# Interleaving the first two pairs of chunks and re-timing the queues of an AdaLN-conditioned FFN kernel

## The reference, cut to what matters

```python
def lora_add(base, inp, A, B):          # A, B chosen per sequence
    t = einsum('bri,bni->bnr', A[idx], inp)
    return base + einsum('bor,bnr->bno', B[idx], t) * 0.5
gate = lora_add(x @ W_gate.T, x, A_gate, B_gate)      # 1024 -> 2752
up   = lora_add(x @ W_up.T,   x, A_up,   B_up)
act  = silu(gate) * up
y    = lora_add(act @ W_down.T, act, A_down, B_down)  # 2752 -> 1024
logits = y @ Wg + bg                                  # 8 experts
top2 = top_k(logits, 2)
out = x + mean over the two experts e of relu(y @ W_e[e] + b_e[e])
```

## Time and profile before

| | us |
|---|---|
| median of three runs | 2058.62 |
| profiled execution, its own time | 2062.44 |
| its span from first to last instruction | 2060.6 |
| TensorE busy | 1882.0 |
| DVE, POOL, ACT busy | 1141.9, 1083.1, 744.0 |
| mean granted TensorE clock | 0.954 |

### The profile page before, as it was taken

How to read it: one execution, slowest core, us unless ns; L and a number is a source line. 1 busy time by engine, 2 the same in 40 slices (tenths; PEclk the granted TensorE clock), 3 DMA queues, 4 the chain that set the end, 5 groups by cost and what they waited for, 6 DMA issues and landing times.

```text
span 2060.6 us, 24701 instructions
## 1 busy us (share of the span) xinstructions
PE 1882.0 (91%) x8679; PEld 1560.7 (76%) x8679; DVE 1141.9 (55%) x1355; ACT 744.0 (36%) x1054; POOL 1083.1 (53%) x659
## 2 busy tenths in 40 slices
PE   4789998999798996799999999798989999999997
PEld 3567776778687785688888888687867788888886
DVE  6446766566358675356666666349684744443210
ACT  4333433334344332444444434333331233333332
POOL 5357877674244443245555545144441666666664
PEclk8899999999899998899999999899998899999999
DMA  4256766653457553323343334456563476666653
GB/s 161 81 169 208 239 251 238 239 182 106 161 183 249 197 195 117 118 92 113 100 135 114 113 101 130 152 199 236 199 203 109 145 195 181 182 179 155 156 111 61
DMA packets 118025, 332.67 MB, mean 161 GB/s; under 512 B 13952, under 2 KB 15872, under 8 KB 117760
## 3 DMA queue, kind: packets, MB, share of 16 engines
q1 hardware_dynamic: 99632, 268.06, 37.5%
q0 software_dynamic: 18272, 62.99, 13.1%
HBM read 249.86 MB, written 90.05 MB: 165 GB/s over the span
## 4 chain that ended last, share of the span: by engine, by line
PE 66%; DVE 7%; issue 6%; DMA 6%; POOL 5%; ACT 3%; SPq 0%; ACTq 0%; DVEq 0%; POOLq 0%
PE PS L1571 20%; PE PS L1572 19%; PE PS L1573 19%; DVE FT L1205 3%; DMA brw<-in_bgu,idx_b 3%; PE PS L1878 2%; PE PS L1616 2%; PE PS L1710 1%; DMA ytp<-in_wgb 1%; POOL brw L691 1%; DMA raw<-in_wp 1%; ACT R L970 1%; PE PS L1829 1%; ACT R L849 1%; DVE R L853 1%
## 5 line engine op out<-in xcount | busy, mean ns | idle before, releaser
L1571 PE MATMUL PS<-R,ring 128*128 128x512 f32 (+1 forms) x1800 | 724.9, 403 | 83.6 <-DVE ring L834 30.4
L1572 PE MATMUL PS<-R,ring 128*128 128x512 f32 (+1 forms) x1800 | 715.1, 397 | 0.0
L1573 PE MATMUL PS<-R,ring 128*128 128x512 f32 (+1 forms) x1800 | 714.1, 397 | 0.0
L1571 PEld LDWEIGHTS PS<-R,ring 128*128 128x128 f32 x1800 | 346.8, 193 | 161.4 <-issue 52.8
L1573 PEld LDWEIGHTS PS<-R,ring 128*128 128x128 f32 x1800 | 346.1, 192 | 75.6
L1572 PEld LDWEIGHTS PS<-R,ring 128*128 128x128 f32 x1800 | 347.6, 193 | 66.4
L712 POOL TENSOR_TENSOR ring<-raw,ring 128x1024 fp32r<-128x1024 f32 x78 | 192.5, 2467 | 360.6 <-ACT ring L840 357.5
L834 DVE TENSOR_TENSOR ring<-FT,ring 128x512 fp32r<-128x512 f32 x168 | 164.4, 982 | 180.3 <-ACT ring L830 177.7
L853 DVE TENSOR_TENSOR R<-FT,R 128x1024 fp32r<-128x1024 f32 x70 | 156.5, 2236 | 186.7 <-ACT R L849 186.5
L1571 PE MATMUL PS<-ring,R 128*128 128x512 f32 x592 | 236.0, 399 | 18.3 <-DVE FT L1151 18.3
L1572 PE MATMUL PS<-ring,R 128*128 128x512 f32 x592 | 234.1, 395 | 0.0
(11 more groups left out here) (184 smaller groups left out, 2384.3 us busy)
## 6 DMA issues: line engine op xcount, KB each, us to landing
raw<-in_wp SPq DMA_DIRECT2D x124, 512.0 KB
act_scratch<-FT SPq DMA_DIRECT2D x140, 256.0 KB
FT<-act_scratch SPq DMA_DIRECT2D x70, 512.0 KB, 5.0
raw<-in_we SPq DMA_DIRECT2D x64, 512.0 KB
raw<-wt_scratch SPq DMA_DIRECT2D x40, 512.0 KB
ytp<-in_wgb SPq DMA_DIRECT2D x32, 256.0 KB, 5.3
y_scratch<-FT SPq DMA_DIRECT2D x7, 1024.0 KB, 7.7
ytp<-in_wp SPq DMA_DIRECT2D x20, 256.0 KB
```

Source lines behind the costliest of these rows:

```text
L1571: e.matmul(out_, hi, whi, start=start, stop=False, skip_group_check=True)
L1572: e.matmul(out_, hi, wlo, start=False, stop=False, skip_group_check=True)
L1573: return e.matmul(out_, lo, whi, start=False, stop=stop, skip_group_check=True)
```

## The change

1. *Interleave.* `pos(q, j)` gives product j of pair q its place: pair 0 has places 0, 1, 4, 5, 6, 7, 8 and pair 1 places 2, 3, 9 to 13. `unit` is replaced by `product(g, q, j)` and `first_pairs(g)`. `lora1_in` is split by token half `w`: half 0 after place 1, half 1 after place 4; `TT` is laid out by half, and `t1_hi`, `t1_lo` run once a half.
2. *Adapter output of half 1* moves from product 4 to product 6 of each pair, and `c_add` k = 1 with it; `b_hi` of that half gets the key 4.3 instead of 2.6 after the pair's start.
3. *Opening.* Small constants come first on SP, the raw loads 1 and 2 earlier; POOL mixes the weights and gathers B before `x0_t3` and `x0_t4`.
4. *Keys of the splits.* `w_hi` n - 4.98 (was n - 5.6), `d_hi` and `a_hi` -3.97 and -3.95 (were -5.6, -5.55), `d_lo`, the loads and others later too.
5. *Mix rounds* every 8.7 units from 22 instead of every 7 from 21; `copy_x` moves from pass 0 (four of 512 rows) to pass 1 (16 of 128 rows).
6. *From pairs to stages.* `load_a` starts at 140.3 and waits for the stores of its own pairs only, `a_hi` of the first two at 144.2 and 144.3, the third at 149.4; the down adapter's inputs (`ad_diff`, `ad_hi`, `ad_lo`) at 149.2 instead of 147.2. `lora2_in` of stages 0 and 3 follows the products of its piece, but for the last.
7. *Logits.* `l_step` every 0.88 unit (was 0.55) in stages 2 to 4 and every 0.34 (was 0.3) after; `t2_hi` and `t2_lo` 1.6 units earlier. The PE part starts in the tail of stage 6 (`last2`), and goes on in `first_pairs` with banks 0 to 3 and 7. Pass 1's x T3 and T4 come through `X0[0]` by `load_x1` instead of the raw buffers.

```diff
+def pos(q, j):
+    if q == 0:
+        return [0, 1, 4, 5, 6, 7, 8][j]
+    if q == 1:
+        return [2, 3, 9, 10, 11, 12, 13][j]
+    return 7 * q + j
...
+            if s == 0:
+                e.wait_ge(s_st, 16 * 7 * (g * 10 + 2 * a + 2))
             if jj == 0:
-                e.wait_ge(s_st, st_all(g))
-                e.wait_ge(s_lo, lo_of(g, 146))
+                e.wait_ge(s_lo, lo_of(g, 145))
...
-            sp.add(7.0 * (r + 3) + 0.3, mix_load, r)
-            sp.add(7.0 * (r + 3) + 5.3, mix_store, r)
+            sp.add(22 + 8.7 * r, mix_load, r)
+            sp.add(22 + 8.7 * r + 4.6, mix_store, r)
...
             if o < 32:
-                return stage_end(g, 1) + 0.6 + 0.55 * o
-            return stage_end(g, 4) + 0.6 + 0.3 * (o - 32)
+                return stage_end(g, 1) + 1.5 + 0.88 * o
+            return stage_end(g, 4) + 0.6 + 0.34 * (o - 32)
...
-                pool.add(op(g, 7 * q) - 5.4, mix_w, g, q)
+                pool.add(op(g, 7 * q) - 5.2, mix_w, g, q)
...
-                        key = (op(g, 0) + 0.5 if g else -2.5) if w else op(g, 1.6)
+                        key = (op(g, 0) + 0.5 if g else -5) if w else op(g, 1.9)
...
-            pool.add(-6 + 0.1 * h, x0_t3, h)
-            pool.add(-5.6 + 0.1 * h, x0_t4, h)
+            pool.add(-1.0 + 0.1 * h, x0_t3, h)
+            pool.add(0.5 + 0.1 * h, x0_t4, h)
...
-                            key = op(g, 14 * p) + [[-1.6, 2.6], [0.1, 2.6]][t][w]
+                            key = op(g, 14 * p) + [[-1.6, 4.3], [0.1, 4.3]][t][w] + (w and p == 10)
...
-                key = op_m(g, FIRST_M[s] + 4) + 2.05
+                key = op_m(g, FIRST_M[s] + 4) + 0.45
                 act.add(key, t2_hi, g, w)
...
+            def product(g, q, j):
+                bk = 4 * (q % 2)
+                ec = g * 85 + 4 * q
+                n = pos(q, j)
+                e.wait_ge(s_lo, lo_of(g, n))
+                if j == 0:
+                    if q >= 2:
+                        e.wait_ge(s_c, g * 85 + 4 * (q - 1))
+                    elif g:
+                        e.wait_ge(s_ev, 28 * g)
+                    m = main1(g, n, "B11", bk, True, True)
+                elif j == 1:
+                    m = main1(g, n, "B21", bk + 1, True)
+                    if q >= 2:
+                        m = lora1_out(g, q, 0, 0, bk + 1)
+                elif j == 2:
+                    if q == 1:
+                        e.wait_ge(s_t1l, 4 * g + 2)
+                    m = main1(g, n, "T1", bk + 2, True, True)
+                elif j == 3:
+                    e.wait_ge(s_ec, ec + 1)
+                    m = main1(g, n, "T2", bk, False, True)
+                elif j == 4:
+                    e.wait_ge(s_ec, ec + 2)
+                    m = main1(g, n, "B22", bk + 2, False)
+                    if q < 2:
+                        m = lora1_out(g, q, 0, 0, bk + 1)
+                elif j == 5:
+                    e.wait_ge(s_ec, ec + 3)
+                    m = main1(g, n, "T3", bk, False, True)
+                else:
+                    if q == 1:
+                        e.wait_ge(s_t1l, 4 * g + 4)
+                    main1(g, n, "T4", bk + 3, True)
+                    lora1_out(g, q, 0, 1, bk + 2)
+                    e.wait_ge(s_ec, ec + 4)
+                    lora1_out(g, q, 1, 1, bk)
+                    m = lora1_out(g, q, 1, 0, bk + 3)
+                m.then_inc(s_pe, 1)
...
+            def first_pairs(g):
+                product(g, 0, 0)
+                if g:
+                    sum2(g - 1, 3)
+                    turn2(g - 1, 4)
+                    turn2(g - 1, 5)
+                product(g, 0, 1)
...
+                lora1_in(g, 0)
+                product(g, 1, 0)
...
+                product(g, 1, 1)
+                product(g, 0, 2)
+                lora1_in(g, 1)
+                for j in range(3, 7):
+                    product(g, 0, j)
+                for j in range(2, 7):
+                    product(g, 1, j)
```

More of the change, by code:

```diff
@@ L558, in build @@
             sp.add(keys[i], load, i)
-        for h in range(2):
-            sp.add(op_m(0, 33) + 0.1, load_x1, h)
+        for o, key in (("T2", op_m(0, 33) + 0.1), ("T3", op(1, 0) + 1.0), ("T4", op(1, 0) + 3.4)):
+            for h in range(2):
+                sp.add(key + 0.02 * h, load_x1, o, h)
         for j in range(70):
```

344 lines of the change are left out of this document (162 added, 182 removed).

## The result

The changed kernel takes 1970.72 us (median of four runs, 1966.76 to 1976.86), the kernel before 2058.63 beside it: a ratio of 0.9575 [0.9547, 0.9604]. It is faster by 88 us where 141 were forecast, and it lies 0.7 us above the upper end of the range. The profiled execution took 1973.38 us with a span of 1971.6; before, 2062.4 and 2060.6.

The account below looks back on a forecast made before the run. Few long TensorE waits (178.6 us idle) and the lower clock they bring were taken as the bound. Terms 14 + 34 + 33 + 43 + 14 + 3 = 141 took profiled 2062.4 to 1921.4, median 1918; range 1885 to 1970.

Parts of the forecast that it names:

- The opening: Start of pass 0: 49 us lost before, 35 left after the new order, so 14 us saved; bounds -22 to +16.
- The copies of x: Moved into pass 1, hidden by early raw loads: nothing taken; if each cost 1.5 us, 23 us.
- the slower case: `c_add` 1 to 3 bunch behind product 6 and product 3 waits in every pair: 2118 us, chance 0.05.
- Pass 0's pairs: Twelve `e_copy` waits and the lower clock lose 48 us; 10 idle and 4 by clock left: 34 us saved.
- round 7: Mix round in pass 0's pairs, ahead of `mix_act` and `mix_w`: holds `w_hi` and `e_copy` about 4 us.
- The check on pass 1: Pass 1's pairs from 900 to 1280 us lose 1.8 us, so neither DVE nor POOL is too slow.
- Nine of the twelve waits are under 3.6 us and go: Pass 0's pairs: `b_hi` of half 1 at key 4.3, 4.6 us later, removes nine `e_copy` waits.
- the rival that mixing stays the bound: Pass 0: rounds still hold POOL and SP, opening gains nothing, 14 and 29 us fall away: 1961, chance 0.14.
- Pairs to stages: From pair 20 to the stages: 34.7 us lost to `e_copy`, the half pair's copy and clock; 1 left, 33 saved.
- Stages: Waits for `t2_lo` and adds plus clock, 54.8 us, 11.4 left: 43 saved; between passes 14, the end 3.
- four steps take 9.6 us instead of 6.0: Stages: at 0.88 a unit, steps outlast a Wg load's 5.3 us, so add waits of 6.5 and 5.6 go.
- Edits with no term: Constants first, banks, later keys of `w_hi`: held to be order alone, with no saving counted.

Follow-up runs that it names:

- e7: Changed kernel with `b_hi` of half 1 back at its old key, 2.6 instead of 4.3: 1993.1 us.
- e1: Changed kernel with the four POOL operations of each mix round cut to 32 of 512 columns: 1927.95 us, with tokens routed otherwise.
- e8: Kernel before with the mix rounds' POOL operations cut to 32 of 512 columns, one round: 2027.59 us, with tokens routed otherwise.
- e5: Changed kernel with the mix rounds at their old places, every 7 units from 21: 1969.02 us.
- e11: Kernel before with only the new keys of the stages' splits (`d_hi`, `a_hi`, `a_lo`): 2026.79 us.
- e9: Changed kernel with the stages' splits (`d_hi`, `a_hi`, `a_lo`) at their old keys: 2049.52 us.
- e18: Changed kernel with the old keys of both the router steps `l_step` and `t2_hi`, `t2_lo`: 1979.85 us.
- e12: Changed kernel with the router steps `l_step` at their old keys, 0.55 and 0.3 a unit: 1974.65 us.
- e4: Changed kernel with `t2_hi` and `t2_lo` at their old place, 1.6 units later: 1969.45 us.
- e3: Changed kernel with stage 5's four adds ahead of the last seven `l_step` and the load of x T2 6 units later: 1959.77 us.
- e17: Changed kernel with only the loads that feed the splits at their old, earlier keys, splits as in the change: 1980.4 us.
- e16: Changed kernel with the old keys of both the stages' splits and the loads that feed them: 1988.21 us.
- e15: Changed kernel with `e_copy` ahead of `w_hi`, stage 5's adds earlier, no `s_ev` wait, `mix_act` 0.6 units later, mix rounds as two jobs: 1970.35 us.
- e14: Changed kernel with `e_copy` ahead of `w_hi`, stage 5's adds before the last steps, no `s_ev` wait, `mix_act` 0.6 units later: 1954.77 us.

## Why the prediction was wrong

**What held.** The opening (12.7 for 14), with the first product at 9.2, the wait behind `w_hi` 9 and 10 and the gather each in its place, though product 4 starts at 58.5 and not 52. Its sum of idle, 28, is 27 by its own terms. Waits named as going: `t2_lo` over 4 us, the half pair's copy, `lt_copy`. The copies of x: pass 1's pairs 2 to 20 take 365.5 us with them and 366.3 without, so nothing is right and the bound of 23 was not needed; with the old key of `b_hi` (e7) the same stretch takes 372.6, though the kernel before, with that key and no copies there, takes 366.3. The expert phase. And `c_add`: no product waits for it, the slower case is out.

**Pass 0's pairs: 10.1 for 34.** Two steps failed. The first is that round 7 "holds `w_hi` and the `e_copy` behind it for about 4 us" and two others cost under 1, the price of the mix rounds. TensorE's waits with ACT standing for a mixed tile went from 1.1 to 15.0 us, and e1, which takes the rounds' work away, brings pair 20 16.7 earlier. The check on pass 1 was read as "neither DVE nor POOL is too slow"; but pass 1 has no rounds. The second is "Nine of the twelve waits are under 3.6 us and go", from "The cause is one". The gather's waits fell from 31.3 to 8.3, but not mainly by the key that was named: e7 puts it back, and they are 12.0. So 24.0 us stay idle, where 10 were forecast, and 15.7 us busy at the lower clock cost 7.8, where 4 were. In the kernel before the rounds were not the main cause: e8 takes their work away there, and 29.7 of 32.4 us of waits stay. It is half of the rival that mixing stays the bound; its other half, no gain in the opening, was wrong. e5 shows that the mechanism given with it, the phase of a round, is not it. How much of the mixed tiles' wait had been hidden behind the gather's, and how much is new, is open.

**Pairs to stages: 24.5 for 33.** That the order on ACT makes these waits held, and they went. But "ACT stood in `a_hi` ... and then in `ad_hi`" leaves out its longest stand, the 8.69 us in `d_hi`, whose key had no term. Each set of edits is enough here without the other: e11 has only the later splits and gains 21.5, and e9, the changed kernel with `d_hi` at its old key, loses nothing (36.9 and 36.5 us from pair 20 to stage 0, against 39.8 and 37.3). "I leave 1" was too little: in product 6 of pair 20 `lora1_out` waits 2.2 us (pass 0) and 2.5 (pass 1) for `b_lo` and 0.7 for `e_copy`, and three stretches at the lower clock, 13.0 us busy, lie in these parts.

**Stages: 42.8 for 60, with the seams.** Three steps failed, in opposite directions. First, the waits for `t2_lo` were counted in full. The spread of steps and the new key, for which most of the 43 were given, do take them away: e18, without both, has 19.8 of the 27.6 back. But together they are worth 9, and alone 4 and 0, which is nothing that can be told.

Second, "four steps take 9.6 us instead of 6.0 ... and they [the waits for adds] go": the adds are waited for elsewhere (5.13 and 5.30 in stage 6, 3.00 for stage 6's own add, and 3.88 in stage 4 of pass 1: 17.3, where 18.3 stood before). By the row of DVE the adds ran at 737.54, 8.6 us after stage 6 had begun, behind the last steps. With the old steps or the old key of `t2_lo` these waits are shorter and `t2_lo` is waited for instead (e12, e4), so DVE owed both; e3, which puts the adds ahead of the steps, gives 11 us back.

Third, "Edits with no term (... later keys of `w_hi`) are order alone". The keys of the splits and of the loads that feed them are worth 17.5 us together. In the kernel before, those of the splits alone are worth 35 (by landmarks 15 in the stages, 21.5 ahead of them), and in the changed kernel old splits with new loads cost 79. So a good part of the sum came by accident: one cause was counted too high and another not at all.

By the rule of the Trainium skill (SBUF — State Buffer, "SBUF: two separate sides"), that a DVE operation with two SBUF inputs and one of POOL exclude each other, the prediction worked out 4 to 8 us less for this term. The trace agrees with the rule: the step at 725.38 took 2.87 us while POOL's `d_lo` ran from 724.85 for 2.87, and those at 728.19 and 728.80, with no such operation on POOL, took 0.68. It points to the right side, but is a small part of the shortfall.

**The signs.** `e_copy` waits over 4.5 us between 100 and 450 were to be absent; there are two, 4.58 and 5.57. Fewer than 12 stretches at the lower clock were named; there are 18. Product 14 was to start at 86 and starts at 90.3; pass 1's first product gained 44, not 100. The last one would by itself have pointed at the middle of the kernel. Of the signs for wrong one came, once: a round followed by a wait of over 5 us (5.57).

**The range.** It had -22 to +16 for the opening, where the cause was plain, and nothing for the edits costed at nothing, where e9 shows 79 us at stake.

**Open.** Of the 42.8 us, 17.5 and 9 have runs behind them, the 9 within overlapping intervals; the rest, by the order between the passes and by what the parts do to each other, was not taken apart. Where e11 gains its 35 is shown, and why for the part ahead of the stages; why 15 more come in the stages is not: the waits for `t2_lo` that I had named stay.

## What to carry to other kernels

A wait shows one cause; before counting it as saved, ask which other instruction would have been late at the same moment, and count only the difference. An edit that only moves the head of an in-order queue has a price as soon as two queues wait for each other: follow the loop load, split, consumer, next load, and compare one turn with what one turn has to feed (here 17.2 us, with two tiles per turn, which feed TensorE for 10.9). What must not come close is a load and the split that waits for it. Here a later split with its load left early gained 35 us (e11), or was 10 worse than with both moved (e17); a later load with its split left early cost 61 (e9 against e16).

## What the runs showed that I had not expected

- Whether an `e_copy` stands ahead of or behind a `w_hi`, 0.06 units apart in their keys, decides over 12 us (0.9501 against 0.9575), a third of them in pass 1's pairs, where hardly a wait is listed.
- Halving a block of POOL work and letting others in between made the kernel 16 us slower by the medians (e15 against e14), with the same operations; one of e15's four runs, at 1955.24, is as fast as e14.
- 19.8 us of waits for `t2_lo` came back in e18 and cost about 9: here half of the wait was paid back by the queue that caught up meanwhile.
